# A fused attention and feed-forward kernel: four of ten score pairs summed on VectorE, six of ten left as two addends to TensorE

## What is computed

```python
def rational_softmax(scores, eps=EPS):
    num = 0.5 * (1.0 + scores * jax.lax.rsqrt(1.0 + scores * scores))
    return num / (jnp.sum(num, axis=-1, keepdims=True) + eps)
h = einsum('bsd,bdh->bsh', x, W[cat_ids]) + b[cat_ids]
q, k, v = (h @ w_qkv.T) split into 16 heads
probs = rational_softmax(causal(q @ k.T * scale - slope * |i - j|))
x = x + (probs @ v) @ w_out.T
# second layer
r = relu(x @ W1[lang] + b1[lang]) @ W2[lang] + b2[lang]
z = layernorm(x + r) * gamma[lang] + beta[lang]
x = x + int8_matmul(round(z / z_scale), weight_int8.T) * z_scale * weight_scale + bias   # z_scale from the largest |z| of all
```

## Time and profile before

| | |
|---|---|
| median of 3 runs | 2266.23 us |
| the profiled execution | 2265.64 us |
| its span (first to last instruction) | 2263.8 us |
| the eight groups, first square of ScalarE to the last | 90.5 to 2138.5 us, 2048.0 us |
| before and behind them | 90.5 us and 125.3 us |
| TensorE busy, mean granted clock | 1803.9 us (80%), 0.907 |
| VectorE busy | 1878.6 us (83%) |
| ScalarE busy | 1685.0 us (74%) |
| GpSimd busy | 1715.7 us (76%) |

### The profile page before, as it was taken

One profiled execution on the slowest core, in us unless ns is written; L12 is line 12 of the kernel. 1 busy time (PEld: TensorE's weight loads), 2 busy tenths in 40 slices (PEclk: granted clock), 3 DMA queues, 4 the chain that ended last, 5 costly groups with the idle time before them and its releaser, 6 DMA issues.

```text
span 2263.8 us, 31228 instructions
## 1 busy us (share of the span) xinstructions
PE 1803.9 (80%) x10640; PEld 904.5 (40%) x10640; DVE 1878.6 (83%) x2114; ACT 1685.0 (74%) x1938; POOL 1715.7 (76%) x784
## 2 busy tenths in 40 slices
PE   5678877877787789998888877877787787887864
PEld 4555323333333346664444433333333333342331
DVE  4358888888889888889789898888888888899768
ACT  0247897989889888889567667999889888767413
POOL 2136887788878887788678887788878887788548
PEclk9899988988898899999999998988988898998879
DMA  5411111110111022202322221110111021121137
GB/s 176 146 49 44 49 30 35 43 45 25 40 40 49 20 69 66 68 25 74 84 77 81 69 54 34 40 49 21 45 40 48 20 79 44 42 62 52 59 123 237
DMA packets 126620, 138.68 MB, mean 61 GB/s; under 512 B 27868, under 2 KB 78044, under 8 KB 126044
## 3 DMA queue, kind: packets, MB, share of 16 engines
q1 hardware_dynamic: 126460, 136.64, 21.5%
HBM read 54.02 MB, written 22.80 MB: 34 GB/s over the span
## 4 chain that ended last, share of the span: by engine, by line
PE 38%; ACT 21%; DVE 20%; issue 12%; POOL 4%; DMA 2%; SPq 2%; DVEq 0%; POOLq 0%; ACTq 0%
ACT yb L669 9%; PE sc L825 7%; PE ov L804 7%; ACT yb L671 7%; DVE gb L1042 6%; PE dn L804 6%; ACT gb L661 6%; DVE gb L983 5%; PE it L723 5%; PE it L740 4%; PE it L747 4%; PE it L727 3%; POOL oT L654 2%; SPq L428 2%; PE it L707 1%
## 5 line engine op out<-in xcount | busy, mean ns | idle before, releaser
L623 POOL TENSOR_TENSOR yb<-yb 128x1024 f32<-128x1024 f32 (+3 forms) x640 | 1510.2, 2373 | 460.9 <-DVE gb L1042 448.6
L669 ACT ACTIVATE yb<-sc 128x1024 f32<-128x1024 f32 (+3 forms) x640 | 566.9, 886 | 376.3 <-PE sc L825 189.8
L1042 DVE TENSOR_TENSOR gb<-sc,yb 128x1024 f32<-128x1024 f32 (+3 forms) x640 | 676.6, 1057 | 186.1 <-ACT yb L671 183.9
L983 DVE TENSOR_TENSOR gb<-gb,yb 128x1024 f32<-128x1024 f32 (+3 forms) x640 | 779.2, 1218 | 3.9 <-ACT gb L661 0.5
L825 PE MATMUL sc<-qmv,kst 128*128 128x512 f32 (+3 forms) x1280 | 505.6, 472 | 295.8 <-DVE gb L1042 278.2
L671 ACT ACTIVATE yb<-yb 128x1024 f32<-128x1024 f32 (+3 forms) x640 | 595.0, 930 | 20.3
L661 ACT ACTIVATE gb<-gb 128x1024 f32<-128x1024 f32 (+3 forms) x640 | 584.1, 913 | 0.1
L825 PEld LDWEIGHTS sc<-qmv,kst 128*128 128x128 f32 x1280 | 238.7, 209 | 648.3 <-DVE gb L1042 453.3
L804 PE MATMUL ov<-gb,vv 128*32 128x512 f32 (+3 forms) x2560 | 338.4, 604 | 18.0 <-DVE den L997 10.5
L804 PE MATMUL dn<-gb,ones 128*32 128x512 f32 (+3 forms) x2560 | 326.3, 584 | 0.0
L723 PE MATMUL it<-hT,wT 128*128 128x512 f32 x496 | 249.9, 629 | 5.8 <-DVE area L921 1.8
(11 more groups left out here) (112 smaller groups left out, 1093.5 us busy)
## 6 DMA issues: line engine op xcount, KB each, us to landing
qmv<-stage SPq DMA_DIRECT2D x384, 64.0 KB
kst<-stage SPq DMA_DIRECT2D x384, 64.0 KB
area<-in_x_dram SPq DMA_DIRECT2D x58, 256.0 KB, 2.8
out_dram<-oT SPq DMA_DIRECT2D x32, 256.0 KB, 3.3
den<-rec_d SPq DMA_DIRECT2D x31, 256.0 KB
wT<-wT_d SPq DMA_DIRECT2D x7, 768.0 KB, 4.4
x_d<-area SPq DMA_DIRECT2D x16, 256.0 KB, 2.6
z_d<-area SPq DMA_DIRECT2D x16, 256.0 KB, 3.2
```

Source lines behind the costliest of these rows:

```text
L623: pool.tensor_tensor(y, y, y, ALU.mult).then_inc(s_y2, 1)
L669: act.activation(y, sc[:, k % SLOTS, :, q0_of(g, k):], ACT.Square).then_inc(s_s2, 1)
L983: dve.tensor_tensor(t, t, yview(k)[:, :, q0:], ALU.add).then_inc(s_num, 1)
L1042: dve.tensor_tensor(gview(k)[:, :, q0:], sc[:, k % SLOTS, :, q0:], yview(k)[:, :, q0:], ALU.mult).then_inc(s_g, 1)
```

## The change

**Fold or split.** Every pair n (0 to 639) is one of two kinds, by a pattern of ten. Four of ten, always the even pair of a unit, are folded: VectorE forms (g+2)·g in place (`fold`, two pairs later), and then, three pairs later, (that + 1) + y² (`numerator`, now a scalar_tensor_tensor); ScalarE has no third step for them. Six of ten are split: GpSimd forms y² and ScalarE (1+g)², one pair later instead of two, and nobody adds them. TensorE multiplies both addends and sums them in PSUM. Of five units four have one folded and one split pair (6 matmuls per bank instead of 4, the two more in the column quarters of heads 2 and 3), and one has two split pairs (8 per bank).

**Rings.** `yb` and `gb` become one buffer of twelve slots, six for each. The slot of y is free after the sum for a folded pair, and only after the products of its unit for a split pair.

**Order.** The products of unit u−3 now stand behind the scores of the even pair. The loops are written out for all eight groups. The items rt, a and zt are emptied by ScalarE instead of VectorE (their largest value is still taken by VectorE, `largest`), with a semaphore of its own; the normalization on GpSimd becomes a multiply-add with one more small instruction for each tile.

```diff
-YRING = 4
-GRING = 8
-NUM_LAG = 2
+ON_ACT = ("rt", "a", "zt")
+RING = 6
+FOLDS = (True, False, True, False, True, False, True, False, False, False)
+SQUARE_LAG = 1
+FOLD_LAG = 2
+SUM_LAG = 3
...
-            if k % 2:
+            if k % 2 == 0:
                 self.events.append(("pv", k // 2 - LAG))
...
         # scalar
+                    if n >= RING:
+                        if folded(n - RING):
+                            act.wait_ge(s_num, folds(n - RING) + 1)
+                        else:
+                            act.wait_ge(s_pv, (n - RING) // 2 + 1)
...
-                    if k >= NUM_LAG or g is not opening:
-                        one_plus_g_squared(G, g, k - NUM_LAG)
+                    if n >= SQUARE_LAG and not folded(n - SQUARE_LAG):
+                        one_plus_g_squared(n - SQUARE_LAG)
...
         # tensor, products
-                pe.wait_ge(s_num, G * PAIRS + 2 * u + 2)
+                for m in (n, n + 1):
+                    if folded(m):
+                        pe.wait_ge(s_num, folds(m) + 1)
+                    else:
+                        pe.wait_ge(s_y2, m + 1)
+                        pe.wait_ge(s_g2, splits(m) + 1)
+                heads = [(h, gview(n + h // 2)[:, h % 2, q0:], True, folded(n + h // 2)) for h in range(HG)]
+                heads += [(h, yview(n + h // 2)[:, h % 2, q0:], False, True) for h in range(HG) if not folded(n + h // 2)]
                 for dst, is_v in ((ov, True), (dn, False)):
-                    for h in range(HG):
+                    for h, weights, begins, ends in heads:
...
         # vector
+            def fold(n):
+                g = gview(n)[:, :, q0_of(n):]
+                dve.wait_ge(s_g, n + 1)
+                dve.scalar_tensor_tensor(out=g, in0=g, scalar=2.0, in1=g, op0=ALU.add, op1=ALU.mult).then_inc(s_fold, 1)
+
+            def numerator(n):
+                g = gview(n)[:, :, q0_of(n):]
+                dve.wait_ge(s_fold, folds(n) + 1)
+                dve.wait_ge(s_y2, n + 1)
+                dve.scalar_tensor_tensor(out=g, in0=g, scalar=1.0, in1=yview(n)[:, :, q0_of(n):],
+                                         op0=ALU.add, op1=ALU.add).then_inc(s_num, 1)
...
+                    if n >= RING:
+                        dve.wait_ge(s_pv, (n - RING) // 2 + 1)
```

More of the change, by code:

```diff
@@ L152, in __init__ @@
         self.operands = [job.name for job in self.items if job.name[0] in ("q", "k")]
-        assert len(self.items) % BANKS == 0 or not has_next
+        self.ranks, self.evacs = ranks(self.items)
+        assert not has_next or len(self.items) % BANKS == 0 and all(eng == "dve" for eng, _ in self.ranks[-BANKS:])
     def item(self, *name):
@@ L207, in runs @@
     def runs(b):
-        return [(0, opening if b == 0 else joining, 1), (1, plain, NG - 2), (NG - 1, ending if b == B - 1 else closing, 1)]
-    starts, n = {}, PRO
+        return ([(0, opening if b == 0 else joining)] + [(hg, plain) for hg in range(1, NG - 1)] +
+                [(NG - 1, ending if b == B - 1 else closing)])
+    starts, n = {}, (PRO, PRO, 0)
     for b in range(B):
-        for hg, g, count in runs(b):
+        for hg, g in runs(b):
             starts[b, hg] = n
-            n += count * len(g.items)
-    REST = n
+            n = tuple(v + w for v, w in zip(n, (len(g.items), g.evacs["dve"], g.evacs["act"])))
+    REST, REST_DVE, REST_ACT = n
     PRO_JOBS = woven(cond_jobs, range(TT))
     END_JOBS = woven(after_jobs, range(DONE, KB), KB - DONE)
+    END_ITEMS = [job for job in END_JOBS if job.parts]
+    END_RANKS, END_EVACS = ranks(END_ITEMS)
     PLACES = 2 + KB - DONE
@@ L227, in tiles_in, with for_groups @@
         return 1 if a >= 2 else (B * KB - (KB - DONE)) // 2
-    def for_groups(eng, body):
+    def for_groups(body):
         for b in range(B):
[L232 to L237, removed]
+            for hg, g in runs(b):
+                body(b, hg, b * NG + hg, g, starts[b, hg])
     with ExitStack() as ctx:
@@ L411, in ops_before, with zs_before @@
             return 2 if g is opening else 2 * NC * G + 3
+        def zs_before(b, j):
+            order = [job.name[1] for job in (ending if b == B - 1 else joining).items if job.name[0] == "zt"]
+            n = KB * b
+            return n + (order.index(j - 2) + 1 if j >= 2 else 0)
         @block.sync
@@ L675, in _ @@
             act.wait_ge(s_chain, 9)
             act.wait_ge(s_wst, 48)
-            for_groups(act, group)
-            for k in range(-NUM_LAG, 0):
-                one_plus_g_squared(B * NG, plain, k)
+            for_groups(group)
+            for n in range(TOTAL - SQUARE_LAG, TOTAL):
+                if not folded(n):
+                    one_plus_g_squared(n)
+            for job, (eng, rank) in zip(END_ITEMS, END_RANKS):
+                if eng == "act":
+                    after(B - 1, job, REST + job.index, 0)
@@ L1079, in output_prev @@
                 dve.tensor_scalar(den[:, :], dn[:, :], SOFT_EPS, None, ALU.add).then_inc(s_out, 1)
-            for_groups(dve, group)
-            for k in range(-NUM_LAG, 0):
-                numerator(B * NG, plain, k)
+            for_groups(group)
+            for n in range(TOTAL - SUM_LAG, TOTAL):
+                if folded(n):
+                    if n >= TOTAL - FOLD_LAG:
+                        fold(n)
+                    numerator(n)
             output_prev(B * NG, NG - 1, -1, NC - 1)
```

278 lines of the change are left out of this document (169 added, 109 removed).

## The result

The changed kernel takes 2643.94 us (median of 4, 2643.04 to 2646.2), the kernel before 2265.88 us beside it (median of 4). The ratio is 1.1669, 95% interval 1.1654 to 1.1684: 378 us slower. The forecast was slower, 2366 us in a range of 2230 to 2450: the direction was right, the size was not, and the time lies outside the range.

What follows compares the result with a forecast made beforehand. Plain groups were bound by ScalarE, VectorE and the score slot; after the change TensorE binds: 2014 us of work at 94% full is 2142 us. By group that is +100, so 2266 + 100 = 2366 us, range 2230 to 2450.

Steps and rivals of the forecast that it cites:

- The products double: TensorE's products go from 2 column turns a unit to 4, 1.78 to 3.56 us, 484 us in all.
- Rival B: Faster: added matmuls cost less than a second turn; priced by number, some 2223 us; chance 0.17.
- 94%: TensorE's assumed filling of the groups, 6% idle: 2014 us of work take 2142 us.
- the lower end: TensorE only 90% full, from ring waits: 2237 us for the groups, +189 us.
- I take the clock as full: TensorE's clock taken as full, since the closing group had 0.99 at 93% busy.
- The wait of the square: ScalarE's even-pair square waits for products in one unit of five: some 2 us more, 17 us a group if unfilled.
- rival C: TensorE sets the pace and the square's waits add up through later pairs: +170 us, 2434 us; chance 0.10.
- The multiplication's wait: VectorE's even-pair multiplication needs a slot freed by unit u−3's products; about half a microsecond of TensorE idle a unit.
- Clock: Sign of being right: TensorE's granted clock at 0.97 or more in the plain groups.
- Price nothing: ScalarE's relief, 205 to 176 us busy in a plain group, given no price because it is off the path.
- the relief of the other engines: Less work on the other engines, given as reason to take 6% TensorE idle instead of the closing group's 6.8%.
- the sum's price: VectorE's fold priced like its old sum, 1218 ns, the upper choice of 541 to 624 us for folds and sums.

Runs made afterwards that it cites:

- e6: e5 with both pairs of a unit of one kind, still four of ten pairs folded: 2785.03 us.
- e9: e6 with the fold one pair and the sum two pairs after the multiplication: 2537.15 us.
- e14: Changed kernel with five of ten pairs folded instead of four, so every unit has one folded and one split pair: 2527.73 us.
- e5: Changed kernel with the products of unit u-2 behind the odd pair's scores, instead of unit u-3 behind the even pair's: 2500.34 us.
- e7: Changed kernel with LAG = 2 instead of 3, fold one pair and sum two pairs after the multiplication instead of two and three: 2460.84 us.
- e13: Changed kernel, LAG = 3 kept, with the fold one pair and the sum two pairs after the multiplication: 2681.43 us.
- e10: e7 with the second addend of split pairs left out on TensorE, so no right output: 2248.88 us.
- e2: Changed kernel, LAG = 3 kept, with the second addend of split pairs left out on TensorE, so no right output: 2347.11 us.
- e11: Kernel before, loop written out, with one pair of four folded: 2548.07 us, ratio 1.1251.

## Why the prediction was right in sign and wrong in size

**TensorE's work** (right). "The products double": 3.57 us a full unit at the full clock, predicted 3.56, whether six or eight matmuls go to a bank. 470 us of work were added in the groups, predicted 484; each group's work was met within 4 us. By number of matmuls it would have been 36 us a group instead of 59. e6 and e9 show with equal counts that the work follows the turns: 16 instead of 20 take 23 to 28 us off. Rival B falls.

**The share of the time in which TensorE works** (wrong, the step that failed). The prediction took 94% from the closing group of before, with 90% as the lower end; it is 82%. 2000 us of work at 94% would be 2128 us, 299 us less than measured. Two terms of it were mis-sized. The idle of TensorE was put at 6%, 128 us, and is 319: 191 us more. And "I take the clock as full" priced the clock at nothing, where busy time at less than the full clock costs 108 us. The 93% and the clock of 0.99 of the closing group were reached with slots of `gb` given back before the asking pair's scores, and with blocks half as long. After the change they did not carry over: the closing group itself reaches 280 of 307.6 us, 91%, the plain ones 79 to 80%. (The stages of the forecast as listed add up to +104 us, not +100; that is no part of the miss.)

**The rings** (right in mechanism, too small by far). The wait of the square was laid out as 2 us in one unit of five, "17 us a group if nothing fills them", which went into the lower bound and, by half, into rival C, but not into the forecast. e14 takes this wait away and gains 116 us, 14.5 a group, so most of the 17. The multiplication's wait was priced at half a microsecond a unit; in the third group it is 47.4 us in 23 places, 2 us each. What it costs by itself no run shows. Together the rings cost 144 us by e5, 183 between the change and e7, and 221 between e13 and e7. Rival C was this, had 2434 us and a chance of 0.10, and is nearest to what happened, 210 us short of it; its sign, squares that wait more than 20 us a group for products, came true with 30.4.

The 378 us as a chain of runs: all of the change but the second addend and the ring waits, 2266 to 2249 (e10), −17; second addend, one edit, 2249 to 2461 (e7), +212; LAG = 3, one edit, 2461 to 2681 (e13), +221; fold and sum a pair later each, −37. In another order the parts differ, since they act on each other: with the late sums and LAG = 3 the second addend costs 297 us (e2 to the change). The waits end with the block of products in front, so longer blocks make them longer: VectorE's wait in the third group is 26.4 us in e2 and 47.4 in the change.

**Clock** (right in direction, wrong in level). 0.93 to 0.94 in the plain groups, predicted 0.97 or more, up from 0.86 to 0.89. In the timeline above TensorE has the low clock after it had stood for 2.90 us; in e7, whose ring waits are gone, the plain group has 0.97. Both point to the gaps of the ring waits as what lets the clock fall.

**ScalarE and VectorE** (right). ScalarE 183 us in a plain group (predicted 176), VectorE's folds and sums 569 us (541 to 624). (The prediction writes that ScalarE loses 0.6 of its third step; it keeps 0.6, and the 234 us less are reckoned rightly.) "Price nothing" held for ScalarE: it was no bound. That the relief of the other engines lets TensorE fill its time better, the reason for 94% rather than 93%, did not hold: in e10 it is worth 17 us in all, and nothing in the third group.

**Groups.** Plain +40 to +46 us (predicted +4), closing +68 (+60), joining +54 (+22), opening +51 (+6), ending +37 (0). In the closing group, where TensorE was full before, the added work alone tells the loss nearly right; where it had room, the added work would have fitted in, and most of the loss is idle time.

What stays open is the rest: in e7's third group TensorE still stands for 28 of 249 us, and no run took the two score slots or the place of the items in TensorE's list apart.

## What to carry to other kernels

The small matmuls that run side by side here are paid by the fullest quarter of the columns and not by their number: before a sum is moved into PSUM, count the turns of each quarter. When a ring gets shorter, look at where its release stands in the releasing engine's own list. If it stands behind the instruction that feeds the asker, a wait can be as long as the block in between, and a bound by busy time alone misses it. And take a filling of 93%, and the clock that goes with it, only from a stage that has the same waits.

## What the runs showed that was not expected

VectorE and GpSimd seem to take turns, not to slow each other evenly. In the changed kernel GpSimd's square of a full pair takes 1.89 us when nothing of VectorE with two SBUF inputs is near, and 2.81 us when such an instruction (a fold, 1.22 us) has begun just before:

```profile
802.01 1.89 POOL L664 TENSOR_TENSOR ring<-ring 128x1024 f32<-128x1024 f32 x1 [3.67 <-DVE ring L1140]
...
810.04 1.22 DVE L1071 SCALAR_TENSOR_TENSOR ring<-ring 128x1024 f32<-128x1024 f32 x1
810.21 2.81 POOL L664 TENSOR_TENSOR ring<-ring 128x1024 f32<-128x1024 f32 x1 [2.62 <-DVE ring L1140]
```

And in the kernel with a quarter folded, where GpSimd's squares follow without a gap, a sum takes 1.77 us and the fold 2.91:

```profile
789.57 11.30 POOL L630 TENSOR_TENSOR yb<-yb 128x1024 f32<-128x1024 f32 x4 [2.30 <-DVE gb L1060]
...
794.51 1.77 DVE L996 TENSOR_TENSOR gb<-gb,yb 128x1024 f32<-128x1024 f32 x1
...
799.04 2.91 DVE L1001 SCALAR_TENSOR_TENSOR gb<-gb 128x1024 f32<-128x1024 f32 x1
```

2.91 us is about one whole square (1.89) and 1.0 more; 2.81 is 1.89 and 0.92, and the fold that began at 810.04 had 1.05 us left when the square began. That is what one would see if an instruction of one engine had to end before that of the other begins. The same shows before the change (lengths at the least, in the median and at the most, all widths):

```profile
L983 DVE TENSOR_TENSOR gb<-gb,yb x640: 412/1215/2899, 99.1 to 2141.1; 128x1024 f32<-128x1024 f32 x128, 128x512 f32<-128x512 f32 x32
...
L1042 DVE TENSOR_TENSOR gb<-sc,yb x640: 406/1215/1227, 93.9 to 2139.4; 128x1024 f32<-128x1024 f32 x128, 128x512 f32<-128x512 f32 x32
```

The old sum, with two SBUF inputs, reaches 2899 ns; the multiplication, which reads PSUM and SBUF, never takes more than 1227. The page "GPSIMD Engine Reference" of the Trainium skill, section 1, names contention of the two for instructions with two SBUF inputs, without a figure. So "the sum's price" of the prediction was a price of the neighbour too and moves with it: a full fold and sum take 1.30 and 1.29 us in the change, and a fold of full width 2.87 us in e11. No run was made of this alone, and the reading rests on these durations.
